# The product with W2 of a fused attention and feed-forward kernel: seven block products in place of eight, from the second sequence on

## The reference

```python
x = x + attn(layernorm(x), ...)            # small latent attention, causal, 64 features
x = x + ffn(layernorm(x), W1, W2, W3)

def ffn(x, W1, W2, W3):                    # W1, W3: 2048 x 512, W2: 512 x 2048
    hidden = silu(x @ W1.T) * (x @ W3.T)   # 1024 x 2048 for each sequence
    hidden = fwht(hidden)                  # Hadamard transform, 2048 wide
    return hidden @ W2.T
```

## Time and profile before

| | |
|---|---|
| median of three runs | 2095.05 us |
| the profiled execution, first to last instruction | 2093.3 us |
| TensorE busy | 2049.4 us, 98% |
| VectorE busy | 1399.0 us, 67% |
| ScalarE busy | 932.7 us, 45% |
| GpSimd busy | 215.0 us, 10% |
| moved by DMA | 278.62 MB, 133 GB/s |

### The profile page before, as it was taken

One profiled execution on the slowest core, in us unless ns is written; L12 is line 12 of the kernel. 1 busy time (PEld: TensorE's weight loads), 2 busy tenths in 40 slices (PEclk: granted clock), 3 DMA queues, 4 the chain that ended last, 5 costly groups with the idle time before them and its releaser, 6 DMA issues.

```text
span 2093.3 us, 26809 instructions
## 1 busy us (share of the span) xinstructions
PE 2049.4 (98%) x9846; PEld 986.1 (47%) x9846; DVE 1399.0 (67%) x2674; ACT 932.7 (45%) x1431; POOL 215.0 (10%) x196
## 2 busy tenths in 40 slices
PE   6889999999999999999999999999999999999999
PEld 3534444444444444444444444444444444444444
DVE  7897878667676666766677576766767666743333
ACT  5866455354444444453444444344443445322221
POOL 2354641101001000001001010010100110000000
PEclk8999999999999999999999999999999999999999
DMA  8644246441463333733345423643246332463211
GB/s 336 227 166 174 97 153 153 160 145 60 121 189 111 137 107 95 176 124 116 116 129 161 141 77 106 170 135 130 69 148 154 125 122 92 118 155 108 91 63 68
DMA packets 231138, 278.62 MB, mean 133 GB/s; under 512 B 178016, under 2 KB 178144, under 8 KB 225632
## 3 DMA queue, kind: packets, MB, share of 16 engines
q1 hardware_dynamic: 231008, 276.91, 42.7%
HBM read 194.81 MB, written 39.85 MB: 112 GB/s over the span
## 4 chain that ended last, share of the span: by engine, by line
PE 91%; DVE 4%; ACT 2%; issue 1%; DMA 1%; SPq 0%; POOL 0%; ACTq 0%; DVEq 0%; POOLq 0%
PE PF L926 18%; PE PF L928 17%; PE PF L927 17%; PE PD L988 10%; PE PD L990 10%; PE PD L989 10%; PE XY L747 1%; PE XY L733 1%; PE XY L734 1%; PE XY L757 1%; PE XY L758 1%; PE XY L679 1%; PE XY L678 1%; DMA PT<-Pl 0%; DVE WS L1909 0%
## 5 line engine op out<-in xcount | busy, mean ns | idle before, releaser
L926 PE MATMUL PF<-XF,WS 128*128 128x512 f16 x1778 | 675.3, 380 | 4.1 <-DVE XF L1915 1.9
L928 PE MATMUL PF<-XF,WS 128*128 128x512 f16 x1778 | 673.9, 379 | 0.0
L927 PE MATMUL PF<-XF,WS 128*128 128x512 f16 x1778 | 673.9, 379 | 0.0
L1344 ACT ACTIVATE SH<-PF,afs 128x512 f32<-128x512 f32 x256 | 175.9, 687 | 516.8 <-PE PF L928 514.8
L988 PE MATMUL PD<-W2S,H 128*128 128x512 f16 x1024 | 388.1, 379 | 0.0
L989 PE MATMUL PD<-W2S,H 128*128 128x512 f16 x1024 | 388.1, 379 | 0.0
L990 PE MATMUL PD<-W2S,H 128*128 128x512 f16 x1024 | 388.1, 379 | 0.0
L926 PEld LDWEIGHTS PF<-XF,WS 128*128 128x128 f16 x1778 | 173.8, 98 | 221.6 <-issue 31.0
L928 PEld LDWEIGHTS PF<-XF,WS 128*128 128x128 f16 x1778 | 174.0, 98 | 209.8
L927 PEld LDWEIGHTS PF<-XF,WS 128*128 128x128 f16 x1778 | 174.3, 98 | 186.2 <-issue 4.8
L1950 DVE SCALAR_TENSOR_TENSOR SH<-PF,afs,SH 128x512 f32<-128x512 f32 x256 | 188.8, 747 | 96.8 <-ACT SH L1344 95.0
(11 more groups left out here) (328 smaller groups left out, 2005.2 us busy)
## 6 DMA issues: line engine op xcount, KB each, us to landing
WS<-wscr SPq DMA_DIRECT2D x112, 896.0 KB, 4.9
W2S<-w2scr SPq DMA_DIRECT2D x30, 1024.0 KB, 6.5
ring<-x SPq DMA_DIRECT2D x56, 256.0 KB, 7.1
wscr<-WS SPq DMA_DIRECT2D x16, 896.0 KB, 4.1
out<-ring SPq DMA_DIRECT2D x56, 256.0 KB, 2.3
RAW<-w13t SPq DMA_DIRECT2D x16, 512.0 KB, 4.1
xraw<-xT SPq DMA_DIRECT2D x28, 256.0 KB, 5.4
XF<-w SPq DMA_DIRECT2D x13, 512.0 KB, 18.5
```

The source lines that it names most:

```text
L926: pe.matmul(bank, wh, th, start=i < 2 and j == 0, stop=False, skip_group_check=True)
L927: pe.matmul(bank, wh, tl, start=False, stop=False, skip_group_check=True)
L928: m = pe.matmul(bank, wl, th, start=False, stop=j == 1, skip_group_check=True)
L1344: ac.activation(SH[:, i, :], PF[:, (1 - k % 2, 2)[i], :], ACT.Silu, scale=afs[:, k % NH:k % NH + 1]).then_inc((a_sb, a_sc2)[i], 1)
```

## The change

From group 4 on (`QF = 4`: the second to the eighth sequence) the product with W2 is made by seven block products. The features of a group are taken as pairs of steps, an even one in `SH` and an odd one in the new buffer `SHO`; two blocks of features by two halves of the tokens are the four blocks of the left matrix, and W2 has four blocks too (two blocks of features by two halves of the 512 outputs). VectorE makes four sums of a pair (`form_sum`), 512 columns each. The seven left forms of a pair, 512 tokens each, get high and low parts in four passes (`parts_high`, `parts_low`), three of 1024 columns and one of 512. `low_part` and `high` are no longer called for these groups.

TensorE runs `unit(q, u)`, 14 for each group: form u // 2, token half u % 2, two token tiles, two pairs, three matmuls of 256 columns. They stand after products 1, 3, 4 and 6 in odd steps and after products 1, 3 and 6 in even steps. Ten of the 14 banks are evicted by VectorE (`add_unit`), either into the rows or into a float32 buffer `TT`; four are copied to `TT` by ScalarE (`take`). GpSimd adds `TT` to the rows (`row_add`), 12 instructions of 512 columns for each group.

The seven right forms of W2 lie in a new scratch tensor `w2f`. Three are blocks of W2, stored by 24 more DMAs in the first sequence; four are sums, made in eight passes in the first two sequences (`load_halves`, `halves_sum` on GpSimd, `sums_high`, `sums_low`, `store_sums`). `load_form2` loads one form (256 KB) at a time into three buffers. The stores of the finished rows come in the fifth and sixth step of the next sequence instead of the second to the fifth. Two scale factors (powers of two) are moved between the parts, some semaphores are merged, and the first sequence's product with W2 stays as it was.

```diff
+QF = 4
+UNITS = {0: (1, 3, 6), 1: (1, 3, 4, 6), 2: (1, 3, 6), 3: (1, 3, 4, 6)}
+UNIT0 = {0: 0, 1: 3, 2: 7, 3: 10}
+P1, P6, P2, P4, P7, P5, P3 = range(7)
+HFORM = ("A11", "S2", "A12", "A22", "S3", "S1", "S4")
+SPLITS = (("A11", "S3"), ("S1", "S2"), ("A12", "A22"), ("S4",))
...
+            def unit(q, u):
+
+                i, g, n = u // 2, u % 2, form_no(q, u // 2)
+                bank = PD[:, u % 2, :]
+                w.wait_ge(v_lo, split_no(2 * q + 1, SPLIT_OF[HFORM[i]]))
+                w.wait_ge(d_wf[n % 3], 16 * (n // 3 + 1))
+                if u >= 2:
+                    sem, no = emptied(q, u - 2)
+                    w.wait_ge(sem, no(q, u - 2))
...
+                for tp in range(2):
+                    for r in range(2):
+                        th, tl = (part_of(q, r, HFORM[i], m)[:, (2 * g + tp) * 128:(2 * g + tp + 1) * 128] for m in range(2))
+                        wh, wl = (WR[n % 3][:, r, m, :] for m in range(2))
+                        o = bank[:, tp * 256:(tp + 1) * 256]
+                        pe.matmul(o, th, wh, start=tp == 0 and r == 0, stop=False, skip_group_check=True)
+                        pe.matmul(o, th, wl, start=False, stop=False, skip_group_check=True)
+                        m = pe.matmul(o, tl, wh, start=False, stop=r == 1, skip_group_check=True)
+                m.then_inc(p_u, 1)
...
-            for i in (-1, 0, 2, 1, 3, *range(4, 16)):
-                down(4 * NK + i)
+            for u in range(14):
+                unit(NK // 4 - 1, u)
...
+            def take(q, u):
+
+                w.wait_ge(p_u, unit_no(q, u))
+                if u >= 10:
+                    w.wait_ge(g_r, grow_no(q, 2, u % 2))
+                elif q > QF:
+                    w.wait_ge(g_r, grow_no(q - 1, 3, u % 2))
+                ac.activation(TT[:, u % 2, :], PD[:, u % 2, :], ACT.Copy, scale=afs[:, 65:66]).then_inc(a_T, 1)
...
+            def parts_low(p, i):
+                w.wait_ge(a_hi, split_no(p, i))
+                w.wait_ge(v_S, sum_no(p, (0, 2, 2, 3)[i]))
+                ve.tensor_tensor(parts_at(p, i, 1), parts_from(p, i), parts_at(p, i, 0), ALU.subtract).then_inc(v_lo, 1)
...
+                ve.tensor_tensor(o, a, b, op).then_inc(v_S, 1)
...
                 fill(k, 0)
-                if k:
+                if k and k <= 4 * QF:
                     low_part(k - 1)
+                if k > 4 * QF and k % 2:
+                    form_sum(k // 2, 0)
+                if k > 4 * QF + 1 and k % 2 == 0:
+                    form_sum(k // 2 - 1, 1)
+                    form_sum(k // 2 - 1, 2)
+                if k > 4 * QF + 2 and k % 2:
+                    parts_low((k - 3) // 2, 3)
+                add_at(k - 1, 6)
                 fill(k, 1)
                 if k:
                     sum_c(k)
                     out_rows((k - 1) // 4 - 1, 2 * ((k - 1) % 4) + 1)
+                if k > 4 * QF + 1 and k % 2 == 0:
+                    parts_low(k // 2 - 1, 1)
+                add_at(k, 1)
+                if k > 4 * QF and k % 2 and k != 4 * QF + 3:
+                    parts_low(k // 2, 0)
                 fill(k, 2)
+                if k > 4 * QF + 1 and k % 2 == 0:
+                    parts_low(k // 2 - 1, 2)
+                    form_sum(k // 2 - 1, 3)
...
+                add_at(k, 3)
                 fill(k, 4)
                 out_rows(k // 4 - 1, 2 * (k % 4))
+                add_at(k, 4)
                 hidden(k, 1)
...
+            def row_add(q, i, g):
+
+                t = TT[:, g, :].rearrange("p (t c) -> p t c", t=2)
+                w.wait_ge(*((a_T, tcopy_no(q, g)), (v_T, tadd_no(q, 2 + g)), (v_T, tadd_no(q, 8 + g)), (a_T, tcopy_no(q, 10 + g)))[i])
...
+                    r = out_part(q, a, b, g)
+                    gp.tensor_tensor(r, r, t, ALU.add).then_inc(g_r, 1)
```

More of the change, by code:

```diff
@@ L149, in d_no, with unit_at, unit_no, form_no @@
     return 8 * q + t + 1
+def unit_at(k, j):
+    q = k // 4 - 1
+    if q < QF or j not in UNITS[k % 4]:
+        return None
+    return q, UNIT0[k % 4] + UNITS[k % 4].index(j)
+def unit_no(q, u):
+    return 14 * (q - QF) + u + 1
+def form_no(q, i):
+    return 7 * (q - QF) + i
+def tcopy_no(q, u):
+    return 4 * (q - QF) + {0: 0, 1: 1, 10: 2, 11: 3}[u] + 1
+def tadd_no(q, u):
+    return 4 * (q - QF) + {2: 0, 3: 1, 8: 2, 9: 3}[u] + 1
+def radd_no(q, u):
+    return 6 * (q - QF) + {4: 0, 5: 1, 6: 2, 7: 3, 12: 4, 13: 5}[u] + 1
+def grow_no(q, i, g):
+    return 12 * (q - QF) + (0, 2, 4, 8)[i] + (1, 1, 2, 2)[i] * (g + 1)
+def split_no(p, i):
+    return 16 + 4 * (p - 2 * QF) + i + 1
+def sum_no(p, i):
+    return 4 * (p - 2 * QF) + i + 1
 def norm2_slots(a):
@@ L402, in taken, with sh, entry, part_of @@
             return (v_pl, part_no(a, 3, groups(a) - 1)) if a > 1 else (p_tr, group_no(1, 3, 1))
+        def sh(k):
+            return SHO if k >= 4 * QF and k % 2 else SH
+        def entry(q, kind, form):
+            return PLACE_B[form] if kind else PLACE_A[form][q % 2]
+        def part_of(q, kind, form, m):
+            e = entry(q, kind, form)
+            return HX[:, m, :] if e == 16 else HN[:, e, m, :]
+        def parts_at(p, i, m):
+            fs, q = SPLITS[i], p // 2
+            if len(fs) == 1:
+                return part_of(q, p % 2, fs[0], m)
+            a, b = (entry(q, p % 2, f) for f in fs)
+            return HN[:, a:b + 1:b - a, m, :]
+        def parts_from(p, i):
+            return (SH[:, :, :], SH[:, :, :], SHO[:, :, :], SHO[:, 0, :])[i]
+        def parts_free(p, i):
+            q, kind = p // 2, p % 2
+            if q == QF:
+                return (p_d, d_no(q - 1 if kind else q - 2, 7))
+            n = 0
+            for f in SPLITS[i]:
+                two = kind == 0 and PLACE_A[f][0] != PLACE_A[f][1]
+                old = q - 2 if two else q - 1
+                if old >= QF:
+                    n = max(n, unit_no(old, 2 * HFORM.index(f) + 1))
+            return (p_u, n) if n else (p_d, d_no(QF - 1, 7))
+        def out_part(q, i, j, g):
+            s = q // 4
+            a = 2 * s + i
+            r = home(a, 2 * g)
+            rows2 = ring[:, r:r + 2, :] if r < 16 else WX[:, g * 1024:(g + 1) * 1024].rearrange("p (t c) -> p t c", t=2)
+            return rows2[:, :, j * 256:(j + 1) * 256]
+        def emptied(q, u):
+            return ((a_T, tcopy_no), (v_T, tadd_no), (v_r, radd_no), (v_r, radd_no), (v_T, tadd_no), (a_T, tcopy_no), (v_r, radd_no))[u // 2]
         def cuts(w):
@@ L411, in build_kernel @@
         d_w2 = [sem(f"d_w2{q}") for q in range(4)]
-        d_x = [sem(f"d_x{r}") for r in range(20)]
+        d_x = [sem(f"d_x{r}") for r in range(8)]
         d_xT = [sem(f"d_xT{k}") for k in range(8)]
@@ L655, in _ @@
                         store_w2(i)
-            for t in range(8):
+            for n in range(7 * (NK // 4 - QF) - 4, 7 * (NK // 4 - QF)):
+                load_form2(n)
+            for t in (4, 5, 0, 1, 6, 7, 2, 3):
                 store(NS - 1, t)
@@ L1104, in _ @@
                     if i in DOWN_AT:
-                        down(4 * k + DOWN_AT.index(i) - 1)
+                        if k < 4 * QF + 4:
+                            down(4 * k + DOWN_AT.index(i) - 1)
+                        if k == 4 * QF + 3 and i == DOWN_AT[-1]:
+                            down(4 * k + 3)
+                    if unit_at(k, i):
+                        unit(*unit_at(k, i))
                     f = 7 * h + i
@@ L1496, in fill @@
                     split2(SPLIT_AT[f])
+                if s < 2 and f - 4 in TPREP[s]:
+                    sums_high(TPREP[s][f - 4])
                 if s + 1 < NS:
@@ L1552, in _ @@
                     fill(k, 6)
-            high(NK - 1)
+            parts_high(NK // 2 - 1, 1)
+            parts_high(NK // 2 - 1, 2)
+            take(NK // 4 - 1, 0)
+            take(NK // 4 - 1, 1)
+            parts_high(NK // 2 - 1, 3)
+            take(NK // 4 - 1, 10)
+            take(NK // 4 - 1, 11)
         @block.vector
@@ L1953, in low_part, with add_at, sums_low @@
+            def add_at(k, j):
+                if unit_at(k, j) and unit_at(k, j)[1] not in (0, 1, 10, 11):
+                    add_unit(*unit_at(k, j))
+            def sums_low(x):
+                w.wait_ge(a_t, x + 1)
+                ve.tensor_tensor(TOUT[:, :, 1, :], TF, TOUT[:, :, 0, :], ALU.subtract).then_inc(v_tl, 1)
             def low_part(k):
@@ L2165, in _ @@
             hidden(NK - 1, 0)
-            out_rows(NK // 4 - 2, 7)
-            low_part(NK - 1)
-            for t in range(8):
-                out_rows(NK // 4 - 1, t)
+            add_at(NK - 1, 6)
+            form_sum(NK // 2 - 1, 1)
+            form_sum(NK // 2 - 1, 2)
+            parts_low(NK // 2 - 1, 1)
+            parts_low(NK // 2 - 1, 2)
+            form_sum(NK // 2 - 1, 3)
+            add_unit(NK // 4 - 1, 2)
+            parts_low(NK // 2 - 1, 3)
+            for u in (3, 4, 5, 6, 7, 8, 9, 12, 13):
+                add_unit(NK // 4 - 1, u)
         @block.gpsimd
@@ L2241, in _ @@
```

(5 more changed lines are left out.)

250 lines of the change are left out of this document (216 added, 34 removed).

## The result

| | before | after |
|---|---|---|
| median | 2095.07 us (2094.95 to 2095.65) | 2222.05 us (2220.62 to 2224.73) |
| span of the profiled execution | 2093.3 us | 2218.8 us |
| after / before | | 1.0607, 95% interval 1.0592 to 1.0622 |

A forecast was written before the change was run, and what follows sets the result against it. TensorE, busy 98% of the span, was taken as the bound. Its gain -66.3, VectorE stalls +37.4, preparation +4 and the end +8.3 gave -16.6 us on the 2093.3 span, so a 2078 us median; range 2050 to 2108.

The forecast's parts named there:

- VectorE's part: VectorE's added work in even steps delays TensorE 6.5 us a sequence, 37.4 us in all.
- upper bound of 12: Most TensorE delay a sequence, if GpSimd's full 1.48 us delays each even step once more: 69 us in all.
- Its own signs of being wrong: TensorE idling before units or in odd steps, or unit matmuls starting over 0.11 us apart.
- the row of 2.11 against 1.279 us: One 1024-column VectorE operation with two SBUF inputs took 2.11 us beside GpSimd's multiplication, against a mean of 1.279.
- The room: Idle time between VectorE's two sums plus time from the second to product 6: 3.31 us in step 62, need 4.27 or 3.55.
- TensorE's gain, -66.3: W2 units of 256-column matmuls at 0.109 us each save TensorE 2.37 us a group over 28 groups.
- VectorE's new work, 40 us a sequence: Added low parts, sums and evictions make VectorE 40 us busier a sequence, 211 of about 241 us.
- Preparation, +4 within 0 to 15: Eight passes adding W2 blocks in the first two sequences cost 4 us, between 0 and 15.
- The end, +8.3: After the last product, GpSimd's pairs of additions bind: 29 us against 24.3, giving back 8.3 us.
- DMA, nothing up to 5 us: Seven 256 KB loads of W2 forms a group replace one of 1024 KB, costing nothing, up to 5 us.
- The last sequence almost without idle time: Sign expected in the profile after: TensorE hardly idles in the last sequence.
- Rival (b): VectorE's two-input operations and GpSimd's additions delay each other in every even step, 12 us a sequence: 2110 us, chance 0.22.

The follow-up runs named there:

- e1: Kernel after the change, with each of GpSimd's 12 additions a group working on one column per token tile instead of 256: 2152.67 us.
- e2: Kernel after the change, with each GpSimd addition replaced by three fills of zeros that read nothing from SBUF: 2159.94 us.
- e4: Kernel after the change, whole computation, with four units in even steps and three in odd ones: 2207.75 us.
- e12: Kernel after the change, with sums, low parts, GpSimd's additions and pass arithmetic on one column, W2 block forms loaded without small stores: 2055.58 us.
- e6: Kernel after the change, with the arithmetic of the eight preparation passes on one column of each block, DMAs kept: 2204.84 us.
- e7: Kernel after the change, without the 24 small stores of W2 blocks, three forms loaded from other forms' places: 2218.13 us.
- e8: Kernel after the change, whole computation, with the new product only in the last sequence's four groups and passes in the sixth and seventh: 2104.84 us.
- e11: Whole computation against kernel after: new product in last sequence only, last group's additions on VectorE, no small stores, six passes in last sequence: 2105.73 us.

## Why the prediction was wrong

**The step that failed** stands in VectorE's part: "Sum: 0.9 (step 0) +0.5 (2) +0.7 (4) +0.7 (6) +0.4 (8) +1.3 (10) +2.0 (14) = 6.5 us a sequence", and its upper bound of 12. Measured: 25.1. Its own signs of being wrong both came: TensorE waits before units (3.4 us a sequence) and in odd steps (5.4), and middle sequences last 265.2 us instead of 246 to 248. It failed in three ways.

1. *GpSimd's reads were priced at single meetings.* I had the row of 2.11 against 1.279 us and used it for three steps. Measured: 13.6 us of lengthening a sequence. 8.4 of it are meetings with the additions (some 14 a sequence), and 10.1 of the 25.1 us of waits go with them (e1, e2: shown). The other 5.2 are meetings with the bias additions, which the prediction did not have; no run removed those.
2. *Only one consumer was looked at.* The room was read between `sum_c`, `sum_e` and product 6. Of the waits 7.9 us are there. Another 14.9 are at pieces of the attention (9.6), units (3.4), and product 2 (1.9, through ScalarE's copy), whose inputs mostly come out of the same late queue. In steps 10 and 14, where nothing else waits, the sizes were right (1.2 and 1.6 against 1.3 and 2.0); in step 0 and 2 they were 0.9 and 0.5 against 6.6 and 4.2. Odd steps, of which I had read 2 to 5 us of room, still hold 5.4 us of waits. e4 shows that it is the queue: the wait follows wherever the room is taken.
3. *No price for the clock.* The wait of step 0 is followed by the lower level in each middle sequence; 1.6 of the 25.1 us are such matmuls.

The rest by its own terms:

- *TensorE's gain, -66.3.* The spacing of 0.109 us was right. The Trainium skill ("TensorE: Matmul & The Clock Gate", Back-to-back issue gap) has 81 ns for a pair of load and matmul at 128 columns, 25 more than the rows; at 256 columns the units' spacing has no such excess. But not all of the 66.3 was had even with VectorE's load back at its level of before: in e12 the span falls by 40.8 us. Of the 25.5 missing, some 16 are in the five middle sequences, where waits for weights, transposes and small steps of attention are left; whether ScalarE's added work is behind any of it stays open.
- *VectorE's new work, 40 us a sequence.* Right (40.5).
- *Preparation, +4 within 0 to 15.* Measured: 14.1 in the first sequence, and 8.0 in the second by e6's cut, so some 22 in all: above the bound. The small stores, which I had named without a price, cost 4.1 of it (e7; e8's +3.6 and e11's 0 say the same).
- *The end, +8.3.* Measured +6.2, although 3.7 us of matmuls are saved there: some 9.9 are lost. The wait for unit 2, where I had 2.4 us, is 2.25 us; the lower clock behind it, without a price, is about half of 3.4. GpSimd's chain holds back ScalarE's copies, for which units 12 and 13 wait 0.5 and 1.0 us, and leaves 7.8 us from the start of the last matmul to the end, against 3.7 before.
- *DMA, nothing up to 5 us.* No unit of a middle sequence waits for a form of W2 in the trace of after.
- *"The last sequence almost without idle time".* Right but for its first step (112), which has idle times of 1.7 and 3.3 us and lasts 18.27 us. After it the even steps without attention last 12.99 to 13.02 us against 14.24, which is one unit fewer and no wait.
- *Rival (b)* had the right mechanism and sign, with 12 us a sequence where 25 came; no case of mine reached 2222. Its price of 12 had been made from even steps alone.

## What to carry to other kernels

Where one engine has no idle nanosecond and another at 68% feeds it in fixed order, work moved to the second is paid at every consumer of its queue: list all instructions behind each inserted operation and who waits for them, not just the product whose input was moved. Before putting adds on GpSimd beside a VectorE that works on two SBUF inputs, list which instruction will be running when the other begins; the second one was held up by as much as 1.07 us here, also a short one. And look at the meetings of GpSimd's old work with VectorE's new. Cut the added work away in one early experiment (as e12): it tells about what the change can give, here 41 us of a calculated 66.
